# Attention scores over all 128 rows, and the weighted sums of a batch in two pairs

## The reference, cut to what matters

```
q, k, v = split_heads(layernorm(x) @ Wq), split_heads(ctx @ Wk), split_heads(ctx @ Wv)
attn    = softmax(q @ k.T * SCALE)            # per head: 256 x 120
out     = merge_heads(attn @ v) @ Wp + bp
x       = x + out
x       = x + ffn(layernorm(x))               # the second half of the kernel
```

## Time and profile before

| | |
|---|---|
| median of 3 runs | 1019.24 us (1012.32 to 1020.25) |
| span of the profiled execution, first to last instruction | 1016.6 us |
| attention phase in it | about 0 to 515 us; a step takes 14.4 to 14.7 us |
| busy: TensorE / VectorE / ScalarE / GpSimd | 86% / 74% / 50% / 58% |

### The profile page before, as it was taken

One profiled execution on the slowest core, in us unless ns is written; L12 is line 12 of the kernel. 1 busy time (PEld: TensorE's weight loads), 2 busy tenths in 40 slices (PEclk: granted clock), 3 DMA queues, 4 the chain that ended last, 5 costly groups with the idle time before them and its releaser, 6 DMA issues. The chain is left out here.

```text
span 1016.6 us, 20535 instructions
## 1 busy us (share of the span) xinstructions
PE 872.4 (86%) x6067; PEld 699.0 (69%) x6067; DVE 754.7 (74%) x1660; ACT 507.8 (50%) x921; POOL 589.0 (58%) x564
## 2 busy tenths in 40 slices
PE   3899999999999999999621139998799999999995
PEld 2666777677767776776521027988788889999984
DVE  4678887788778877887388965897577777777742
ACT  1356555655565565555246205464355555655541
POOL 4346655765576557565732265456687776676344
PEclk9899999999999999999755568999899999999998
DMA  4355655665566556654232033374566666655433
GB/s 145 114 177 187 213 198 178 203 214 194 182 203 207 199 185 203 209 203 162 95 116 83 3 84 124 105 195 123 140 172 165 171 175 156 156 152 138 122 68 42
DMA packets 129518, 156.55 MB, mean 154 GB/s; under 512 B 22452, under 2 KB 104628, under 8 KB 129352
## 3 DMA queue, kind: packets, MB, share of 16 engines
q1 hardware_dynamic: 104072, 113.08, 34.3%
q0 software_dynamic: 15616, 25.70, 12.1%
q10 hardware_dynamic: 9792, 17.31, 4.6%
HBM read 74.93 MB, written 26.28 MB: 100 GB/s over the span
## 5 line engine op out<-in xcount | busy, mean ns | idle before, releaser
L345 POOL TENSOR_SCALAR XN<-X,mv,rstd 128x256 f32<-128x256 f32 x126 | 152.9, 1221 | 131.3 <-DMA xn_table<-XN 62.8
L578 DVE TENSOR_REDUCE NM<-bank 128x4 f32<-128x480 f32 x256 | 159.8, 656 | 76.6 <-PE bank L733 76.6
L411 ACT ACTIVATE PT<-bank 120x512 f32<-120x512 f32 x256 | 138.9, 596 | 123.7 <-PE bank L758 120.1
L1643 PE MATMUL bank<-W2H,HH 128*128 128x256 f32 x512 | 145.5, 284 | 2.0 <-issue 2.0
L1644 PE MATMUL bank<-W2L,HH 128*128 128x256 f32 x512 | 144.1, 281 | 0.0
L1645 PE MATMUL bank<-W2H,HL 128*128 128x256 f32 x512 | 144.0, 281 | 0.0
L1097 POOL DMA_INDIRECT out_dram<-C,IO x60 | 110.7, 1844 | 50.6 <-issue 31.3
L1372 DVE TENSOR_TENSOR HL<-hf,HH 128x512 fp32r<-128x512 f32 x128 | 87.4, 690 | 51.3 <-ACT HH L1527 50.6
L534 DVE RECIPROCAL RR<-RC 128x256 f32<-128x256 f32 x64 | 111.0, 1736 | 9.6 <-POOL OT L355 9.3
L1522 ACT ACTIVATE hf<-bank,B 128x512 f32<-128x512 f32 x128 | 87.8, 686 | 42.2 <-PE bank L1645 36.5
L733 PEld LDWEIGHTS bank<-KX,QX 128*128 128x128 f32 x512 | 71.5, 192 | 53.0 <-DVE NM L578 26.1
(11 more groups left out here) (189 smaller groups left out, 1788.5 us busy)
## 6 DMA issues: line engine op xcount, KB each, us to landing
QX<-QH ACTq DMA_DIRECT2D x64, 256.0 KB
W<-w1T_dram SPq DMA_DIRECT2D x16, 1024.0 KB, 5.5
W<-w2T_dram SPq DMA_DIRECT2D x16, 1024.0 KB, 5.8
X<-x_dram SPq DMA_DIRECT2D x32, 256.0 KB, 3.1
QX<-QL SPq DMA_DIRECT2D x32, 256.0 KB
XB<-x_dram SPq DMA_DIRECT2D x32, 256.0 KB, 3.1
RC<-PVS SPq DMA_DIRECT2D x64, 128.0 KB, 2.1
OC<-PVS SPq DMA_DIRECT2D x64, 128.0 KB, 2.8
```

What stands on the lines that cost most here:

```text
L345: ins = pool.tensor_scalar(dst[:, t, :], src[:, t, :], mv[:, t, 0:1], rstd[:, t:t + 1], ALU.subtract, ALU.mult)
L411: act.activation(PT[u][0:M, HE * k:HE * (k + 1), :], score_bank(b, k // 2)[k % 2][0:M, :], ACT.Exp, scale=SCALE) \
L578: dve.tensor_reduce(NM[u][:, t, :].rearrange("p (f n e) -> p n e f", n=HN, e=HE)[:, n, :, :], smax_bank[q % 2][:, 0:4 * M].rearrange("p (e ...
L1643: pe.matmul(o, wh, xh, start=first, stop=False)
```

## The change

Three edits. First, each score matmul contracts all 128 rows instead of its half's 64; the zeros in KX make the other half's products zero. Secondly, for this the ones in KX may stand only in the row of the own half, so the start writes them by four DMAs (u and f) where it wrote them by two, and the `ones` tile is [1, 960] instead of [2, 1920]. Thirdly, TensorE's order changes: w0 moves from the end of a step to the next one, and stands in front of w1; m1 moves ahead of s2; w2 moves behind m4, m5 and rows, in front of w3. The order in a step is now rows2, m0, m1, s2, w0, w1, m2, m3, s3, m4, m5, rows, w2, w3, m6, m7, queries, maxima, project, router_logits, keys, s0, values, s1. No other engine's order changes.

```diff
-    ones = sb("ones", [HALVES, H * M], FP32)
+    ones = sb("ones", [1, H * M // HALVES], FP32)
...
         for u in range(2):
-            sp.dma_start(KX[u][MAX_ROW:P:HP, :, :, :, :].bitcast(FP32).rearrange("p n f e m -> p (n f e m)"), ones[:, :]) \
-                .then_inc(ones_moved, 16)
+            for f in range(HALVES):
+                row = HP * f + MAX_ROW
+                sp.dma_start(KX[u][row:row + 1, :, f, :, :].bitcast(FP32).rearrange("p n e m -> p n (e m)"),
+                             ones[:, :].rearrange("p (n r) -> p n r", n=HN)).then_inc(ones_moved, 16)
...
-                            pe.wait_ge(ones_moved, 32)
+                            pe.wait_ge(ones_moved, 16 * 2 * HALVES)
...
                         for f in range(HALVES):
-                            own = slice(HP * f, HP * (f + 1))
-                            ins = pe.matmul(score_bank(b, n)[f][0:M, e * S:(e + 1) * S], KX[u][own, n, f, e, :],
-                                            QX[u][own, HE * n + e, :], start=True, stop=True)
+                            ins = pe.matmul(score_bank(b, n)[f][0:M, e * S:(e + 1) * S], KX[u][:, n, f, e, :],
+                                            QX[u][:, HE * n + e, :], start=True, stop=True)
...
             max_scores(0)
+            max_scores(1)
             scores(2, 0)
-            max_scores(1)
+            weigh(0, 0)
             weigh(1, 0)
             max_scores(2)
             max_scores(3)
             scores(3, 0)
-            weigh(2, 0)
             max_scores(4)
             max_scores(5)
             rows()
+            weigh(2, 0)
             weigh(3, 0)
             max_scores(6)
             max_scores(7)
...
             scores(0, -1)
             values()
             scores(1, -1)
-            weigh(0, -1)
```

## The result

The change made the kernel slower: 1034.72 us median of 4 runs (1032.76 to 1040.37), against 1018.66 us for the kernel before (4 runs, 1012.32 to 1020.25). The ratio is 1.018 with a 95% interval of 1.013 to 1.022. The forecast was 1029 us, 10 more than before; it is 16 more. The sign and the range were right, the size was about two fifths too small.

A forecast was written before the change was run, and what follows sets the result against it. The ring from m0 through w1, PVS copy, SyncE's queue and low queries was taken to bound the kernel; later w1 and QL give steps of 14.98 and 14.79, +0.35 x 31 = +10.9, so 1029 us, range 1018 to 1040.

The forecast's parts named there:

- Q: The forecast ring: m0, w1, PVS copy, SyncE's queue, low queries, next m0; mean step 14.89 us against 14.54.
- R: Not in the prediction: ring s0, two exps, s1, two exps, s2, then TensorE's order to next s0; 15.23 us after.
- What bounds the kernel before: The ring through SyncE's queue sets the step, 14.65 us; TensorE's speed enters only in the first 1.24.
- Breaks and TensorE's bill: TensorE per step: fewer shape changes -0.80 us, wide scores +0.1, paired w -0.2; sum -0.9, unless the ring shortens none counts.
- m0 to w1: TensorE at the head of a step: m1, s2 and w0 now stand ahead of w1, 1.24 to 1.57 us, +0.33.
- s1 behind s0: TensorE's score groups: s0 to s1 grows from 1.77 to 1.87 us; TensorE still reaches m0 at 14.6, just ahead of the moves.
- VectorE's path: m4 and m5 wait for maxima, m6 0.7 us later, QL ready at 10.96; second kind of step 14.79 against 14.42.
- Slower still, TensorE becomes late too: Rival: shared DMA engines or restarts after waits at m4, m5, s1; step 15.3, +24, 1043 us; chance 0.12.
- Faster: Rival: TensorE sets the step at m0, so -0.9 us a step arrives in the time, 991 us; chance 0.06.
- No change: Rival: SyncE's queue hops shrink or w pairs run tighter, the ring grows by 0.1 us; 1016 to 1023; chance 0.19.
- the queue's stretch: SyncE from row sums to low queries: forecast unchanged at 8.05 or 7.72 us in the two kinds of step.
- Step to time: Mean step +0.35 us times 31 steps gives +10.9 us; filling and draining steps may take off 2.

The follow-up runs named there:

- halves wait apart: Changed kernel, with the two score matmuls of each half waiting only for their own bank's exp: 1031.9 us, ratio 1.014 to the kernel before.

## Why the prediction was right, and where it was short

- *Which ring.* The number fell into the range although another ring than the forecast one set the step; that is in part luck. Not luck is that Q by itself gave what was forecast: with R eased ("halves wait apart") the step is 14.93, against a forecast 14.89. The prediction lacked R. Its own numbers could have shown it: s1 at 5.84 + 0.56 + 7.3 = 13.70 after m0, s2 not before 13.70 + 1.87 = 15.57, which is 0.68 after an m0 at 14.89, where it put s2 at 0.55.
- *What bounds the kernel before:* right. Q held every second step; moving the store behind the low queries took those steps from 14.72 to 14.41.
- *Breaks and TensorE's bill:* the changes of shape are four a step, as counted. (One working there is off: 0.56 less 0.20 over four matmuls is 0.09, not 0.11. That stretch has a break only ahead of it, and 0.56 less 4 x 0.11 leaves 0.12 for it; the 0.20 comes from the lone m1.) A wide score in the stream takes 0.12 per matmul, 0.48 instead of my 0.45 (last keys matmul at 311.08, first of values at 311.67, with the four of s0 between). That is 0.06 more than the 0.42 of the packed group with its break. The Trainium skill, "TensorEngine Tiling (Array Packing)", Overview, gives up to twice the speed for a contraction of at most 64 rows. The rows agree with that only for the packed group without its break, 0.22 by estimate (0.42 less 0.20). A w pair takes 1.00 (315.76 to 316.76), 0.43 for the added one, the lower bound, not 0.47. So TensorE's own bill fell by about 0.84 (an estimate: -0.80 + 4 x 0.06 - 2 x 0.14) and none of it reached the time, as forecast; its busy share fell to 95%, where I had 93.
- *m0 to w1, the failed step.* The prediction put s2 at 0.55 after m0 and w1 at 1.57. Measured: 0.75 and 1.86. s2 did not follow m1 but waited for exp(3), 2.00 after s1. Waiting for the halves apart gave exactly 1.57, so the sum was right and the condition wrong.
- *s1 behind s0, the mis-sized term.* I priced the longer hop at 1.87 and looked at s0 to s1 alone. The second matmul of a wide group starts 0.20 to 0.22 after the first and the others 0.12 apart, so the last starts 0.43 to 0.45 after the first, where the two halves side by side needed 0.22. The hop is 1.77 + 0.21 = 1.98. The sum that puts TensorE at m0 at 14.6 also kept the old 1.77 inside its 7.3, without the 0.1 that it had just priced. And s1 to s2, which TensorE's own work had covered with w0 (1.97 of work for 1.77 of exps), lost that cover: w0 had moved behind s2, and the exps asked 1.98. I wrote that w0's absence pays for the later m6; it paid with idle time.
- *VectorE's path.* m4 and m5 wait for the maxima as forecast (m0 to m4 3.64, to m5 4.21), m6 comes at 6.07 instead of 5.84, which is the lateness of s2. QL is ready at 11.19 (forecast 10.96). The waits of m4 and m5 did cost, though through R: putting w2 back gave 0.27.
- *The rivals.* "Slower still, TensorE becomes late too" at 0.12 named restarts after the waits of m4, m5 and s1, and is close to what happened: the measured +16 lies between the forecast's +10 and its +24. Its other cause, high and low queries sharing DMA engines, did not appear: issue to m0 stayed 3.7. "Faster" had the breaks right, but the time they free went into waiting. "No change" did not come: the queue's stretch stayed (7.93 against 7.88 in the mean).
- *Step to time.* +0.35 x 31 was 11; the steady steps gave +0.65 x 31 = 20, filling and draining steps some more, 25 to the end of attention. The two profiled spans differ by 17.7 only, because the rest came out 7.3 shorter; 6.3 of that is less waiting of TensorE for gathered rows. Whether the change causes that or it falls so by chance is open: among the other kernels this wait comes to between 3.0 and 9.5 us.

## What to carry to other kernels

When the profile of one engine shows 98% busy, look for the rings that pass through it and add each one up in rows; what an edit on that engine gives is decided by the longest ring after the edit, and an edit that lengthens two rings must be added up in both. A filler (here w0) between two links of a producer and consumer chain is cover: before it is moved, compare what the chain's round trip needs with the work that is left between its links. Where two banks were handed over together, signalling and waiting for each by itself took 0.7 us off the hop from s0 to s1 and did more than any order tried here.

## What the runs showed of the hardware that I had not expected

- Two groups of four side-by-side fp32 products of 32 columns stream into each other: 1.00 us for both against 0.57 for one, so the second costs 0.43.
- The moves that m0 waits for took longer when a store stood ahead of them in SyncE's queue. The last of them was counted 3.5 to 3.7 us after the issue of the low queries in the kernel before, and 3.0 to 3.1 with nothing changed but the x1 store issued behind them. In the changed kernel it was 3.4 to 3.8, and 2.7 to 2.9 with the later store. The ranges of 20 steps do not overlap, and the size of the move is the same. So the later store gave twice, 0.4 us by the earlier issue and 0.5 by the faster landing (kernel before).
- The experts' phase varied by 7.4 us between profiled executions of the same code, nearly half of what this change does. TensorE's wait for gathered rows accounts for much of it: 9.6 us in the longest of these phases, 3.0 in the shortest.
